# Moving the last weight store behind the first tiles' loads and broadcasts, and the last shared products around the first transposition

## The reference

```python
w = weights[conditions]                               # 128 matrices of 32 x 32
h = jnp.einsum('bct,bcd->bdt', x, w)                  # 4096 tokens of 256
scores = sigmoid(h @ gate_w.T)                        # 32 experts
# two of four groups per token, then the 8 largest of the 16 experts in them
wsel = wsel / wsel.sum(-1, keepdims=True) * 2.5
x_lat = h @ fc1_w.T                                   # 128 latent columns
e = relu2(einsum('tl,eil->eti', x_lat, w1)) * cw.T[:, :, None]
routed = einsum('eti,eli->tl', e, w2) @ fc2_w.T
shared = relu2(h @ shared_up_w.T) @ shared_down_w.T   # 512 inner columns
return x + shared + routed
```

## Time and profile before

| what | value |
|---|---|
| time, median of three runs | 444.12 us (442.39 to 445.01) |
| the profiled execution: first to last instruction | 443.5 us |
| PE busy | 397.0 us, 90% of the span |
| DVE busy | 307.5 us, 69% |
| ACT busy | 253.5 us, 57% |
| POOL busy | 197.5 us, 45% |
| DMA, mean over the span | 211 GB/s |
| granted TensorE clock, mean | 0.941 |

### The profile page before, as it was taken

One profiled execution on the slowest core, in us unless ns is written; L12 is line 12 of the kernel. 1 busy time (PEld: TensorE's weight loads), 2 busy tenths in 40 slices (PEclk: granted clock), 3 DMA queues, 4 the chain that ended last, 5 costly groups with the idle time before them and its releaser, 6 DMA issues. The chain is left out here.

```text
span 443.5 us, 7029 instructions
## 1 busy us (share of the span) xinstructions
PE 397.0 (90%) x2261; PEld 345.9 (78%) x2261; DVE 307.5 (69%) x580; ACT 253.5 (57%) x330; POOL 197.5 (45%) x153
## 2 busy tenths in 40 slices
PE   8798989999989928799999999999999999999920
PEld 8788989999979828588888888888878888888810
DVE  0167997799898823697787887787767888876200
ACT  1274442734654520768778778778776787775310
POOL 5000076746776700006444576552644455434562
PEclk9899996999999968999999999999999999999555
DMA  6991473742752778858999988899998899979532
GB/s 173 251 308 41 144 289 102 239 177 72 239 220 96 223 226 257 261 181 225 210 222 234 200 214 231 222 216 315 329 351 224 231 209 304 358 221 243 111 40 31
DMA packets 66249, 93.55 MB, mean 211 GB/s; under 512 B 19295, under 2 KB 48086, under 8 KB 65622
## 3 DMA queue, kind: packets, MB, share of 16 engines
q1 hardware_dynamic: 52210, 77.71, 54.6%
q0 software_dynamic: 13296, 15.08, 20.1%
q10 hardware_dynamic: 708, 0.32, 0.3%
HBM read 94.48 MB, written 30.18 MB: 281 GB/s over the span
## 5 line engine op out<-in xcount | busy, mean ns | idle before, releaser
L530 POOL DMA_INDIRECT out_x<-res,sid_sb x70 | 122.0, 1742 | 161.9 <-DMA out_x<-res,sid_sb 72.0
L1011 DVE TENSOR_TENSOR act_lo<-act_full,act_hi 128x1024 fp32r<-128x1024 f32 (+3 forms) x92 | 105.9, 1151 | 24.7 <-ACT act_full L874 18.5
L1277 DVE SCALAR_TENSOR_TENSOR scaled<-h_banks,cond_bd 128x1024 f32<-128x1024 f32 (+3 forms) x76 | 86.5, 1138 | 42.3 <-PE h_banks L694 42.0
L694 PE MATMUL h_banks<-xc_hi,w_ring 128*128 128x512 f32 (+3 forms) x304 | 95.4, 396 | 4.0 <-DMA w_ring<-w_dram 1.8
L509 POOL DMA_INDIRECT rows_dram<-payload,slot_idx x64 | 68.6, 1072 | 56.0 <-DVE payload L1152 30.6
L715 PE MATMUL y_banks<-act_hi,w_ring 128*128 128x512 f32 (+3 forms) x304 | 79.3, 384 | 1.5 <-ACT act_hi L872 1.5
L872 ACT ACTIVATE act_hi<-scaled 128x1024 fp32r<-128x1024 f32 (+3 forms) x76 | 74.9, 986 | 2.6 <-PE y_banks L715 1.8
L874 ACT ACTIVATE act_full<-scaled 128x1024 f32<-128x1024 f32 (+3 forms) x76 | 74.7, 983 | 0.0
L715 PEld LDWEIGHTS y_banks<-act_hi,w_ring 128*128 128x128 f32 x304 | 56.7, 195 | 12.5 <-ACT act_hi L872 1.2
L694 PEld LDWEIGHTS h_banks<-xc_hi,w_ring 128*128 128x128 f32 x304 | 52.0, 193 | 16.1 <-issue 4.9
L694 PE MATMUL h_banks<-xc_lo,w_ring 128*128 128x512 f32 (+3 forms) x152 | 57.9, 381 | 0.0
(11 more groups left out here) (147 smaller groups left out, 642.3 us busy)
## 6 DMA issues: line engine op xcount, KB each, us to landing
w_ring<-w_dram SPq DMA_DIRECT2D x76, 512.0 KB
cond_bd<-s_dram SPq DMA_DIRECT2D x64, 512.0 KB, 5.5
w_dram<-w_ring SPq DMA_DIRECT2D x8, 1024.0 KB, 7.4
x_in<-in_x SPq DMA_DIRECT2D x8, 512.0 KB, 6.8
res<-in_experts_raw SPq DMA_DIRECT2D x4, 1024.0 KB, 10.2
out_x<-x_in SPq DMA_DIRECT2D x8, 512.0 KB, 3.8
rows_sb<-rows_dram SPq DMA_DIRECT2D x16, 256.0 KB, 4.8
rows_dram<-in_pad_rows SPq DMA_DIRECT2D x5, 328.0 KB, 4.3
```

The lines of the kernel that those rows point to most:

```text
L530: pool.indirect_dma_start(out, bass.IndirectOffsetOnAxis(ap=sid_sb[:, i % SID_RING, j, GROUP_SIZE:PER_GROUP], axis=0), res[:, i % 2, j * H ...
L694: last = pe.matmul(h_banks[:, s, m * BANK:m * BANK + SIZE[i]], w, v, start=n == 0, stop=n == 2)
L1011: dve.tensor_tensor(lo, full, hi.bitcast(f32), ALU.subtract).then_inc(act_lo_ready, 1)
L1277: dve.scalar_tensor_tensor(pair(scaled, i, u), h, 0.0, scale, ALU.max, ALU.mult).then_inc(scaled_ready, 1)
```

## The change

On SP, `store_split(3)` moves from before `load_sid(0)` to behind `load_scale(0, u)`, directly ahead of `splits_stored(1)`. `read_table(1)` moves ahead of `load_sid(0)`, and `read_group(1)` ahead of `load_scale(0, u)`. On PE, `shared_down(14)` moves ahead of `transpose_s(0)`, and `shared_down(15)` ahead of `transpose_x(0)`. No instruction is added or taken away, and no wait is changed.

```diff
             for u in range(PAIRS):
                 load_weights(0, u)
-            store_split(3)
+            read_table(1)
             sp.wait_ge(pads_stored, GROUPS * DMA)
             sp.wait_ge(dummy_stored, DMA)
             sp.wait_ge(rows_scattered, scatters(BATCHES - 1))
             load_sid(0)
             load_rows(0)
-            read_table(1)
             load_sid(1)
             load_rows(1)
             store_shared(6)
+            read_group(1)
             for u in range(PAIRS):
                 load_scale(0, u)
-            read_group(1)
+            store_split(3)
             splits_stored(1)
             for u in range(PAIRS):
                 load_weights(1, u)
@@
             shared_down(13)
             shared_up(15)
+            shared_down(SHARED_UNITS - 2)
             transpose_s(0)
-            shared_down(SHARED_UNITS - 2)
+            shared_down(SHARED_UNITS - 1)
             transpose_x(0)
-            shared_down(SHARED_UNITS - 1)
             experts_up(0, 0)
```

## The result

| | before | after |
|---|---|---|
| median of four runs, us | 443.25 (441.49 to 445.01) | 449.59 (448.08 to 452.58) |
| ratio of the times | 1 | 1.0147, 95% interval 1.0080 to 1.0214 |
| profiled span, us | 443.5 | 446.3 |

The changed kernel is slower by 6.3 us; the forecast was 451.9 with a range of 445.8 to 455.0 (of before, a fourth run has been added beside the three that were known).

A forecast was written before the change was run, and what follows sets the result against it. PE bounds the tiles, which get going when tile 2's scales have landed (177.35 us before). That landing 7.4 us later plus 0.4 for the clock gives +7.8 on the median 444.1: 451.9 us, range 445.8 to 455.0.

The forecast's parts named there:

- Up to the first transposition: SP issues tile 0's scales' load at 157.6 instead of 157.92; transpose_s(0) starts at 160.4, 4.1 us sooner.
- at no price: Tile 1's rows and scales and block 6's store move some 4 us forward into an idle queue; nothing waits for them.
- The stores in line: The two 1 MB stores queue behind tile 0's broadcasts, landing at 179.3 us; forecast case, chance 0.77.
- the upper bound: Stores' landing: broadcasts land until 173.0, then two megabytes at 3.2 us each, at 179.3.
- rival B: Stores don't queue behind the broadcasts: they land after 7.8 us at 174.2, time 446.5; chance 0.11.
- The estimate by the Trainium skill: Broadcasts and stores as one 4.2 MB transfer: 11.6 us from 164.6, landing at 176.2, end at about 448.7.
- What stands behind the wait: After SP's wait for the stores, tile 2's scales land at 184.8 against 177.35: +7.4 us; PE's gain becomes waiting.
- The clock: PE resumes at the lower clock after waiting for tile 2's scales: 0.4 us lost, bounds nothing and 2.6.
- Rival D: PE stays at 1.2 GHz through much of tile 0: 454 to 457 us; chance 0.06.
- C's point: Rival of no slowdown, 444.5 us: the wait costs nothing if both stores land by about 171.9; chance 0.06.
- From there to the end: After tile 2's scales' transposition, the rest takes as long as before, so the shift reaches the end undiminished.

The follow-up runs named there:

- sp_only: The changed kernel with PE's order as before, so SP's part of the change alone; 448.85 us against 442.14 of before, ratio 1.0166.
- pe_only: The kernel before with only the change's two moves on PE, SP's list as before; 442.50 us against 442.14 of before, ratio 1.0035.
- scales_ahead: sid_ahead with tile 2's rows and tile 1's first two broadcasts also ahead of the wait for the stores; 437.63 us against 443.47 of before, ratio 0.9886.
- both: The changed kernel with store_split(3), then table reads and scales' loads of tiles 2 and 3, moved ahead of tile 0's broadcasts; 440.48 us against 443.47 of before.
- sid_ahead: The changed kernel with table reads and scales' loads of tiles 2 and 3 moved ahead of store_split(3) and its wait; 442.10 us against 442.14 of before.

## Why the prediction was right

Step by step, from the common start (the prediction's times less 155.01, the trace's less 152.34):

| step | predicted | measured |
|---|---|---|
| load of tile 0's scales issued | 2.6 | 2.6 |
| `transpose_s(0)` | 5.4 | 5.2 |
| first broadcast issued | 9.6 | 10.1 |
| last store landed | 24.3 | 24.2 |
| load of tile 2's scales issued | 27.0 | 27.1 |
| `transpose_s(2)` | 29.8 | 29.6 |
| the same, less before (22.3) | +7.4 | +7.2 |

*Up to the first transposition.* Right: SP got no earlier, the load landed 2.5 us after its issue (2.8 assumed, 6.6 before). From the transposition to the first broadcast went 5.0 us instead of the 4.2 of before, and so the first broadcast came 0.5 us later than forecast. The scales' store was in flight beside tile 1's rows (issued at 157.41) and the shared block's store (158.00), which the forecast had set down at no price; that these cost it the 0.8 us is not shown.

*The stores in line.* Right, and the decisive choice: they landed 9.7 and 11.4 us after their issue instead of 4.6 and 7.1. From the first broadcast's issue to the last store's landing went 14.0 us (165.1 + 11.4 - 162.47); 14.7 was forecast from the upper bound, 9.6 would have been the lower one (rival B). That these 0.7 us and the 0.5 us above nearly cancel, so that the landing came within 0.1 us, is luck. The estimate by the Trainium skill, page "DMA: Bandwidth & Descriptors", section "Anatomy of one DMA", whose fit is for POOL's path, was 11.6 us: too short by 2.4.

*What stands behind the wait.* Right: 27.1 - 24.2 = 2.9 us from the landing to the load of tile 2's scales (2.7 assumed), and what PE had gained, 4.3 us at the first transposition and 7.3 at `experts_up(0, 0)`, went into the third one's wait.

*The clock.* The sign was right, the size 0.1 us instead of 0.4: from `transpose_s(2)` to `transpose_s(4)` 24.5 us against 24.4 before. Busy time by stretch of the changed kernel:

```profile
165.00:170.00 5.00, 1.18 (x6) 0.63 (x4) 2.45 (x2) 0.12 (x1) 0.00 (x0) 1.00 0.99 297
170.00:175.00 5.00, 0.00 (x0) 0.00 (x0) 0.00 (x0) 0.00 (x0) 0.00 (x0) 0.65 1.04 404
175.00:180.00 5.00, 0.00 (x0) 0.00 (x0) 0.00 (x0) 0.00 (x0) 0.00 (x0) 0.50 0.16 62
180.00:185.00 5.00, 3.08 (x8) 2.39 (x9) 0.00 (x0) 1.93 (x3) 0.00 (x0) 0.50 0.37 62
185.00:190.00 5.00, 4.35 (x21) 3.28 (x20) 4.17 (x4) 4.31 (x6) 0.00 (x0) 0.98 0.99 342
```

PE idled from 166.2 to 181.9 us. It fell to the lower level on the way, at about 171.5 us, and stood there up to about 185 us, 3 us after it had resumed; the matmuls of that stretch filled gaps in which before it had waited for ACT and DVE (0.7 and 1.0 us). Rival D didn't come, and C's point (stores landed by 171.9, which is 16.9 behind the common start) was missed by 7 us.

*From there to the end.* At `transpose_s(4)` the shift is still +7.4 us; at the end of these two executions it is 5.5. Of the missing 1.9 us 1.8 are a loss in the execution of before, not a gain in the other: two of its tiles took 13.6 and 14.9 us (from 308.4 to 336.8 us), where the others took 13.3, with PE waiting for weights:

```profile
322.93 0.74 PE L694 MATMUL h_banks<-xc_hi,w_ring 128*128 128x512 f32 x2 [0.71 <-DMA w_ring<-w_dram]
```

sp_only has one such tile too (14.6 us), pe_only and scales_ahead one of 14.0 each, the changed kernel has none. So the forecast of +7.8 is to be compared with +7.4 in the tiles; of the medians' +6.3 the interval reaches from 3.5 to 9.5 us, and 7.4 lies in it.

## What to carry to other kernels

A wait in an engine's list is free only as long as what it waits for is long done; moving a bulk transfer to just ahead of its own wait makes everything behind that wait late by the transfer and by all that stands in the queue ahead of it. When a load is moved forward, follow not the instruction that waited but the last of the loads that the stage needs, here tile 2's 18 KB, and look for it behind every wait of the list. The cure was to leave the stores in the queue and take what the next tiles need out from behind the wait: with that the same change is 1.1% faster than the kernel before (some 5 us, of which the traces show 2.8 at this place).

## What was not expected of the hardware

**Behind the stores SP itself is slower.** In the kernel before, with the 2 MB of stores in the queue, the issue of a scales' load took 1.15 us, and 0.68 in the changed kernel with nothing of SP ahead; two register loads took 2.6 us behind the stores in the kernel named both and 2.9 in the kernel before (from 160.54 to 163.47), against 1.4 us elsewhere. A long queue alone is not the reason: in sid_ahead, with 2.1 MB of broadcasts ahead in the same queue, two register loads took 1.4 us (165.33 to 166.68), and two scales' loads with two more register loads between them 2.49 us, as in the kernel before with its stores landed (2.50). What it is about the stores these runs don't tell.

**A longer wait of PE can cost less by the clock than a shorter one.** After 15.7 us of idling the changed kernel lost 0.1 us up to `transpose_s(4)`: the level had fallen during the wait and rose 3 us after PE had resumed. pe_only, with 5.2 and 3.0 us of idling, was still at 1.00 when it resumed at 174.2 us, fell at about 175.4, rose at about 182.3 and lost 1.6. So it matters when the level falls, and not only for how long PE has waited. What decides this the runs don't tell: in the first part the same idle times were followed by a clock of 0.66 in one execution (70 to 80 us) and of 1.00 in another.
